# Half as many, wider reads of queries and keys, and three steps moved into the opening of an attention block

## The reference

```
mod = (silu(c) @ wmod).reshape(B, 6, 1, 256)            # shift, scale, gate for each half
sa, ca, ga, sb, cb, gb = mod[:, 0] ... mod[:, 5]
ga, gb = sign * maximum(|.|, 0.25)
h = layernorm(x) * (1 + ca) + sa
Q, K, V = h @ W_qkv.T + b_qkv, per head                 # 16 heads of 16
attn = softmax(causal(Q K^T / 4))
x = x + ga * ((attn V) @ W_o.T + b_o)
h = layernorm(x) * (1 + cb) + sb
w = softmax of the two best of h @ gate_w
x = x + gb * sum over the two best experts of w_e * (silu(h @ w1[e]) @ w2[e])
```

## Time and profile before

| | |
|---|---|
| median of 3 runs | 1039.14 us (1035.15 to 1039.42) |
| profiled execution | 1042.76 us, of which span 1041.0 us |
| busy share of PE, DVE, ACT, POOL | 88%, 70%, 56%, 34% |
| mean granted TensorE clock | 0.955 |
| DMA, mean | 106 GB/s, 110.61 MB |

### The profile page before, as it was taken

How to read it: one execution, slowest core, us unless ns; L and a number is a source line. 1 busy time by engine, 2 the same in 40 slices (tenths; PEclk the granted TensorE clock), 3 DMA queues, 4 the chain that set the end, 5 groups by cost and what they waited for, 6 DMA issues and landing times.

```text
span 1041.0 us, 19379 instructions
## 1 busy us (share of the span) xinstructions
PE 920.5 (88%) x6174; PEld 539.6 (52%) x6174; DVE 729.0 (70%) x2342; ACT 578.0 (56%) x1258; POOL 357.2 (34%) x305
## 2 busy tenths in 40 slices
PE   6798799998899999989999988778599999999990
PEld 3343445333445334544443444322498889999880
DVE  6689676879666889657789676894536675444598
ACT  3245285766585777486676647558434543434452
POOL 1521011242423125224103333003577456655530
PEclk7899799999999999999999998889899999999996
DMA  8345246236316256254365473106213323222689
GB/s 275 117 63 123 75 61 137 51 48 139 70 25 135 47 92 137 67 71 104 57 114 117 106 167 110 33 25 188 51 49 118 99 66 106 77 77 67 197 279 307
DMA packets 83171, 110.61 MB, mean 106 GB/s; under 512 B 15866, under 2 KB 56370, under 8 KB 83074
## 3 DMA queue, kind: packets, MB, share of 16 engines
q1 hardware_dynamic: 75442, 89.45, 36.9%
q0 software_dynamic: 6816, 18.62, 5.6%
q10 hardware_dynamic: 816, 1.32, 0.4%
HBM read 69.42 MB, written 35.41 MB: 101 GB/s over the span
## 4 chain that ended last, share of the span: by engine, by line
PE 58%; DVE 16%; ACT 10%; issue 6%; DMA 3%; POOL 3%; SPq 3%; another core or an unknown queue 0%; POOLq 0%; ACTq 0%; DVEq 0%
PE PO L1603 9%; PE PH L1484 9%; PE PY L1484 8%; PE PS L1583 7%; PE PM L1560 6%; ACT PR L973 4%; DVE MXF L1277 3%; PE PHT L1687 3%; PE PX L1615 2%; PE PX L1529 2%; DVE JK L1274 2%; SPq L673 2%; PE PS L1587 1%; DMA LD<-OS 1%; PE PX L1538 1%
## 5 line engine op out<-in xcount | busy, mean ns | idle before, releaser
L973 ACT ACTIVATE PR<-PS 128x512 f32<-128x512 f32 (+3 forms) x768 | 334.8, 498 | 162.1 <-PE PS L1587 125.7
L1274 DVE CUSTOM_DVE_ANT_0 JK<-PM,MK 128x128 bf16<-128x128 f32 (+3 forms) x512 | 238.6, 483 | 59.4 <-PE PM L1560 58.8
L1560 PE MATMUL PM<-QK 128*128 128x512 bf16 (+3 forms) x768 | 250.5, 335 | 27.6 <-DVE MXF L1277 15.2
L1583 PE MATMUL PS<-QK 128*128 128x512 bf16 (+3 forms) x768 | 248.5, 334 | 12.1 <-ACT PR L973 11.3
L1277 DVE TENSOR_REDUCE MXF<-PM 128x1 f32<-128x512 f32 x256 | 174.8, 683 | 75.4 <-PE PM L1560 73.8
L1603 PE MATMUL PO<-PR,V 128*17 128x512 f32 (+3 forms) x1536 | 165.2, 503 | 0.0
L1583 PEld LDWEIGHTS PS<-QK 128*128 128x128 bf16 x768 | 74.9, 98 | 173.8 <-ACT PR L973 107.8
L1560 PEld LDWEIGHTS PM<-QK 128*128 128x128 bf16 x768 | 75.5, 99 | 105.8 <-DVE MXF L1277 38.8
L1484 PE MATMUL PH<-W1S,XT 128*128 x426 | 115.2, 406 | 15.1 <-DVE XT L1446 14.0
L1033 ACT ACTIVATE HS<-PH 128x512 f32<-128x512 f32 x71 | 42.5, 598 | 142.2 <-PE PH L1484 136.0
L893 POOL DMA_INDIRECT XL<-H2D,TOK x71 | 80.6, 1135 | 115.2 <-DVE TE L1417 67.8
(11 more groups left out here) (266 smaller groups left out, 1279.8 us busy)
## 6 DMA issues: line engine op xcount, KB each, us to landing
QK<-SD SPq DMA_DIRECT2D x180, 128.0 KB
SD<-SP SPq DMA_DIRECT2D x42, 256.0 KB, 2.8
OP<-OS SPq DMA_DIRECT2D x64, 64.0 KB
LP<-LR SPq DMA_DIRECT2D x64, 64.0 KB
W1S<-in_w SPq DMA_DIRECT2D x8, 512.0 KB, 6.0
W2L<-in_w SPq DMA_DIRECT2D x4, 1024.0 KB, 7.8
X<-XA SPq DMA_DIRECT2D x3, 1024.0 KB, 8.5
H2D<-XA SPq DMA_DIRECT2D x3, 1024.0 KB, 4.6
```

Of the source, the lines that this page charges most:

```text
L973: eng.activation(PR[:, slot, i, c0:512], PS[m % 3][:, c0:512], ACT.Exp, scale=0.25).then_inc(S["exp"].sem, 1)
L1274: eng.tensor_tensor_reduce(JK[:, jk % 2, 0:w], PM[m % 3][:, 0:w], MK[:, 512 - w:512], 1.0, -3.0e38, ALU.add, ALU.max, MXA[:, mb, h, qt:qt ...
L1560: eng.matmul(PM[m % 3][:, 0:128 * (k1 - k0)], QK[:, r, h, 0, qt * 128:(qt + 1) * 128], QK[:, r, h, 1, k0 * 128:k1 * 128], start=True, stop ...
L1583: last = eng.matmul(PS[m % 3][:, c0:512], QK[:, r, h, 1, j * 128:(j + 1) * 128], QK[:, r, h, 0, 512 * f + c0:512 * f + 512], start=True, s ...
```

## The change

**Reads.** `ROWS` now has six entries (queries or keys, first block, count of blocks, first part, whether the parts differ). With one entry two or three blocks of 16 partitions are read at once: where `more` is 1, from parts that follow each other in DRAM; where it is 0, from one part that is repeated (`broadcast_to`, a dimension of step 0). So that a head's number and its row come in an order that allows this, the rows of W_qkv and b_qkv for queries and keys are reordered ahead of the kernel (`by_row`), a pair's row in SD is now number-major, head-minor, and QK is laid out as queries or keys first, then head. The stores, the count of bytes read and the matmuls stay as they are.

```
@@ -72,8 +72,8 @@
 
-ROWS = [(which, n, part) for which, parts in enumerate(((0, 0, 0, 1, 1, 2), (0, 1, 2, 0, 1, 0)))
-        for part in range(3) for n in range(6) if parts[n] == part]
+
+ROWS = ((0, 0, 3, 0, 0), (0, 3, 2, 1, 0), (1, 5, 1, 0, 1), (1, 3, 2, 0, 1), (0, 5, 1, 2, 0), (1, 0, 3, 0, 1))
 
@@ -143,14 +143,17 @@
         place(-3, 0, stats0(half) + [(0, ("mod",))] * (half == 0))
+    place(-3, 0, [(0, step) for _, step in stats(1)[:6]])
     for half in range(2):
...
             place(-3, 1, [(0, ("sd", 0, 0)), (0, ("rep", 0, 0))])
+            place(-3, 1, [(0, step) for _, step in stats(1)[6:8]])
         place(-3, 1, [(0, ("tr", 0, k, half)) for k in range(2)])
...
     place(-3, 1, [(0, ("sd", 0, 1)), (0, ("rep", 0, 1))])
+    place(0, 4, stats(1)[8:])
     for tp in range(4):
@@ -161,7 +164,7 @@
                 place(w + 1, 2 + 2 * tp, one("v", b, tp))
-        if b:
+        if b > 1:
             place(w - 1, 4, stats(b))
@@ -174,9 +177,10 @@
             place(2 * u + 2, 17, one("div", u))
-    place(0, 18, one("mod2"))
-    place(0, 20, one("gates"))
-    place(0, 22, one("bvo"))
+    for i in range(8):
+        place(0, -35, one("mod2", i))
+    place(1, 12, one("gates"))
+    place(0, -20, one("bvo"))
     for b in range(B - 1):
@@ -206,8 +210,8 @@
         for f, n in ((2, NM),) if g else ((0, NM0), (1, NM)):
-            place(g, n // 2 - LEAD, [(0.5 if g and i else 0, ("cmax", g, f, i)) for i in range(f == 0, 6)]
-                  + [(CROW if g else 2, ("crow", g, f))])
+            place(g, n // 2 - LEAD - (f == 0), [(0.5 if g and i else 0, ("cmax", g, f, i)) for i in range(f == 0, 6)]
+                  + [(CROW if g else 1 if f == 0 else 2, ("crow", g, f))])
         if g == 0:
@@ -329,8 +333,8 @@
     "sd": {"sd0": 32, "sd1": 32, "sd2": 32},
-    "rep": {"rep_a": lambda g, half: 192 * (half == 0),
-            **{f"rep{i}": (lambda g, half, i=i: (208 if g >= 3 else 192) * (slot_of(g) == i and half > 0)) for i in range(3)}},
+    "rep": {"rep_a": lambda g, half: 96 * (half == 0),
+            **{f"rep{i}": (lambda g, half, i=i: (112 if g >= 3 else 96) * (slot_of(g) == i and half > 0)) for i in range(3)}},
     "max": {"m": 1, "mx": 1},
@@ -666,12 +670,15 @@
                         sp.wait_ge(S["neg"], 3)
-                        eng.dma_start(QK[96:99, r, :, 0, :], ZR[:, :].unsqueeze(1).broadcast_to([3, 4, T])
+                        eng.dma_start(QK[96:99, r, 0, :, :], ZR[:, :].unsqueeze(1).broadcast_to([3, 4, T])
                                       ).then_inc(S[f"rep{r}"].sem, 16)
-                    for which, n, part in ROWS:
-                        sd_done(sp, u, part, half)
-                        eng.dma_start(QK[16 * n:16 * n + 16, r, :, which, sl],
-                                      SD[u, part, which, r0:r0 + 64, sl].rearrange("(h r) t -> r h t", r=16)
+                    for which, n, count, part, more in ROWS:
+                        parts = slice(part, part + 1 + more * (count - 1))
+                        for k in range(parts.start, parts.stop):
+                            sd_done(sp, u, k, half)
+                        rows = SD[u, parts, which, r0:r0 + 64, sl].rearrange("a (r h) t -> a r h t", r=16)
+                        eng.dma_start(QK[16 * n:16 * (n + count), r, which, :, sl],
+                                      rows if more else rows.broadcast_to([count, 16, 4, sl.stop - sl.start])
                                       ).then_inc(S["rep_a" if half == 0 else f"rep{r}"].sem, 16)
@@ -1485,8 +1492,8 @@
 
-            def mod_columns(WM, cols):
-                for i, col in enumerate(cols):
+            def mod_columns(WM, cols, first=0):
+                for i, col in enumerate(cols, first):
                     for k in range(2):
@@ -1502,11 +1509,15 @@
                 elif kind == "mod2":
-                    pe.wait_ge(S["wm1"], 16)
-                    px_free(pe, step)
-                    mod_columns(WM1, (256, 384, 512, 640, 0, 128, 768, 896)).then_inc(S["px"].sem, 1)
+                    i = a[0]
+                    if i == 0:
+                        pe.wait_ge(S["wm1"], 16)
+                        px_free(pe, step)
+                    last = mod_columns(WM1, (256, 384, 512, 640, 0, 128, 768, 896)[i:i + 1], i)
+                    if i == 7:
+                        last.then_inc(S["px"].sem, 1)
                 elif kind == "gates":
-                    pe.wait_ge(*after("mod2", "mod2"))
+                    pe.wait_ge(*after("mod2", "mod2", 7))
                     px_free(pe, step)
@@ -1726,11 +1737,17 @@
 
+    w_qkv, b_qkv = np.asarray(inputs["L0_attn_W_qkv"]), np.asarray(inputs["L0_attn_b_qkv"])
+
+    def by_row(a):
+
+        return a.reshape(8, 4, 16, -1).transpose(0, 2, 1, 3).reshape(a.shape)
+
     nc = bacc.Bacc("TRN2", target_bir_lowering=False, num_devices=1)
...
         "x": inputs["L0_attn_x"],
-        "wqkvT": np.asarray(inputs["L0_attn_W_qkv"]).T,
-        "b_qk": np.asarray(inputs["L0_attn_b_qkv"])[0:512].reshape(4, 128).T,
+        "wqkvT": np.concatenate([by_row(w_qkv[0:512]), w_qkv[512:768]]).T,
+        "b_qk": by_row(b_qkv[0:512]).reshape(4, 128).T,
         "b_v": np.asarray(inputs["L0_attn_b_qkv"])[512:768].reshape(2, 128).T,
```

## The result

| | before | after |
|---|---|---|
| median | 1039.28 us (4 runs, 1035.15 to 1041.12) | 1183.17 us (4 runs, 1181.81 to 1188.21) |
| ratio | | 1.142 (1.138 to 1.146) |
| profiled execution: span, mean clock | 1041.0 us, 0.955 | 1180.0 us, 0.903 |
| busy share of PE, DVE | 88%, 70% | 79%, 62% |
| share of the DMA queue of SyncE, of 16 engines | 36.9% of 1041 us | 24.8% of 1180 us |

The change makes the kernel 14% slower. The forecast was 1130, with 1057 to 1185; 1.142 of the median that it started from is 1187, at and just over the upper end. The direction and the mechanism came, the size did not: 91 us were forecast, and 144 (or 148 by the ratio) came.

What follows compares the result with a forecast made beforehand. TensorE sets the pace in the middle, VectorE in the first group. 28.6 - 10.4 = 18 us early plus 72 in later windows make 90, taking the profiled 1042.8 to 1133; forecast 1130 on the median's scale, range 1057 to 1185.

Steps and rivals of the forecast that it cites:

- That last step no row shows: New reads: the smaller side's outermost dimension decides, so 3, 2, 2 and 3 engines; a group takes 23.5 us instead of 10.9.
- rival 1: New reads: the smaller side doesn't decide, all 16 engines carry them, only the gains remain, -13 us, 1026; 13%.
- rival 2: Few engines, but a lone one reaches 30 GB/s or more; six reciprocal stalls of about 3 us; 1077, part of the 80%.
- rival 3: Few engines, but VectorE's wait doesn't reach TensorE; only the opening's 18 us remain, 1057; 4%.
- the even windows: Windows 2, 4, ... 12: LP<-LD 12.4 us later each, reciprocal waits; 54 us plus 18 of low clock, 72.
- rival 4: Whole kernel: gains and losses cancel, within 0.5% of before (5 us); 3%.
- the three banks: Even windows: TensorE can run three PSUM banks ahead, about 1.5 us each time, cutting 63 us by 9 to 54.
- the odd ones nothing, since of what VectorE waits for nothing lies behind their reads: Odd later windows: their slower reads cost no time; the later windows' 72 us come from the even ones.
- the reads of groups 0 to 3: Early reads: opening +11.3, group 1 +8.8, altogether 21.6 with the bias product's 1.5; group 2 +11.2.
- the bias product's 1.5: Opening, after 50 us: the moved bias product costs VectorE and TensorE about 1.5 us, not covered.
- the gain of the steps: Moved steps: -10.4 for second modulation part and bias product, -4.2 for sums of sequence 1, +1.5 given back; -13 us.
- the 4.2 us of the sums: First group, where VectorE sets the pace: moving the sums of sequence 1 into the opening saves 4.2 us.

Runs made afterwards that it cites:

- experiment 3: Changed kernel with the same six reads written with the 16 rows outermost from group 1 on, twelve reads for each half of group 0: 0.9931 of before.
- experiment 5: Changed kernel with reads of three blocks cut to two and one, giving four reads of two blocks and four of 16 partitions: 1.1296 of before.
- experiment 6: Changed kernel with twelve narrow reads except wide ones for groups 5, 7, ... 15 (odd windows): 1.035 of before; or for 4, 6, ... 14 (even windows): 1.0727.
- experiment 1: Changed kernel with twelve reads of 16 partitions for its six, new layout and moved steps kept: 0.9952 of before.
- experiment 7: Kernel before with all moved steps: 0.9958; only `mod2`, `gates`, `bvo`: 0.9959; only sums of sequence 1: 0.998; only reordered rows and new layout, twelve reads: 1.0038.

## Why the prediction was wrong in size

**Right: the mechanism of the slow reads.** The smaller of the two outermost dimensions sets the number of engines. LP<-LD 27.6 us behind the first read (28.1), the first maximum at 44.1 (45.85), the seventeenth at 58.9 (61.90), a wait of the reciprocal in six windows (9 to 12 us forecast, 9.5 to 14.9 seen), a DMA share near 0.2 for over 20 us at 50 to 70 GB/s (0.25 at 73): all are in the trace. "That last step no row shows" is now shown by experiment 3, and by the share of 0.13 in experiment 5. All four rivals are out: rival 1 by the share of 0.25, rival 2 by these waits where it had about 3 us, rival 3 by 81 us of the even windows, rival 4 by the ratio.

**Near: the even windows.** They were put at 72 us, 54 of TensorE's waits and 18 of clock. They cost 81 by the ratio and 76 between the two traces of experiment 6, which show the terms: TensorE idle 61 us more, and busy 15 more at the lower clock. VectorE's reciprocal waited 69 us more (73.0 for 4.4) where 63 was forecast, so the three banks gave their credit, 8 us for 9, and the clock cost nearly what it was put at; what was too low is VectorE's wait.

**Wrong: "the odd ones nothing, since of what VectorE waits for nothing lies behind their reads".** This is the step that failed, for 41 of the 57 us that are missing. The question was asked for what stands behind the reads in the queue, and not for the reads' own consumer, TensorE's first maximum of the group. For groups 1 and 2 the forecast did compare landing and due time; for the later groups it did not, though it takes one line: reads go out at place 2 of a window, the group's first maximum stands at place 14 (34 places ahead of its own window, which is the next but one), 12 places are 18.6 us where a window of 24 takes 37.15, and the reads were put at 25.6 with start and landing. That is 7 us late, and 9.2 to 9.9 were seen in windows 3, 7 and 11. There the maximum, less its wait, stood 18.9 us behind the first read and the landing took 28.2 to 28.8. In windows 5 and 9, where the list has layernorm and output steps in these places, it stood 27.4 us behind, and the waits are 0.8 and 1.0. In even windows the reciprocal stands ahead of this maximum in the list, and the trace shows no wait for the reads there.

**Near: the reads of groups 0 to 3.** 21.6 + 11.2 less the bias product's 1.5 is 31 us. The ratios leave 31, the traces show 37.9; that the first agrees to the microsecond is luck. In the trace each group's reads took 2 us more than 25.6 (group 1: issued 65.74, first maximum 93.64), the opening was 3 us later, and group 3's wait of 2.86 us had no term.

**Wrong: the gain of the steps.** -13 us forecast, -4 to -5 measured. The two waits that the move takes away were 8.5 us, but what comes last instead, the read of the row of maxima, is waited for by 1.4 us; `mod2` ahead of the first maximum makes the next row of maxima 2 to 4 us late where the reads are quick; and the 4.2 us of the sums are mostly given back. By the ratios: 9 us of steps, 9 of even windows, 41 of odd ones, less about 2 elsewhere, is 57, with an error of 4 us or so on each of the windows' terms.

## What to carry to other kernels

Before merging DMAs, look at the outermost dimension of both sides as the instruction carries it: two or three blocks put outside a dimension of 16 left three or two engines of 16, to halve a count of issues that nothing waited for. The same merge with the 16 rows outermost and the copies inside keeps all engines. When a transfer becomes slower, compare its landing with its own first reader in every window, before asking what is queued behind it.

## What the runs showed of the hardware that was not expected

- A DMA engine's pace was not one number. 25 GB/s for each of the few busy ones in the kernel after; 9 GB/s for each of 16 with destinations of 16 partitions, whether its runs are 2 KB (144 GB/s) or 8 KB long (142 GB/s, experiment 1); 12 GB/s with 48, 32 and 16 partitions (187 GB/s, experiment 3); 23 for stores to DRAM from 128. The share is near 1 in all but the first, so a share of 1 is no sign of full speed. With all 16 engines at work the reads to 48, 32 and 16 partitions were quicker than those to 16 alone; how much of the 25 is due to fewer busy engines no run separates.
- The issue of a read of half the columns depends on the layout: 12 in 5.62 us with the layout of before (experiment 7, all steps), 7.55 us in the new one (experiment 1). Both have runs of 1 KB and 16 partitions; why is open. The 7.05 of the earlier trace rows are no exception: there one read took 1.88 us to issue and the other eleven 0.43 each.
- A cost of moving `mod2` that was not in the forecast: in the kernel with only `mod2`, `gates` and `bvo` moved, one small operation of VectorE took 3.46 us where its neighbours take 0.17. It began 0.09 us after GpSimd's memset of QK, whose single steps take 3.5 us, and TensorE then waited 3.74 us for a bank:

```profile
38.55 0.17 DVE L1193 TENSOR_SCALAR MS<-MOD 128x16 f32<-128x16 f32 x1
38.66 7.07 POOL L848 MEMSET QK<- 32x4096 bf16 x2 [33.05 <-PE PM L1565]
38.75 3.46 DVE L1195 TENSOR_SCALAR MS<-MS 128x16 f32<-128x16 f32 x1
...
42.94 0.61 PE L1565 MATMUL PM<-QK 128*128 128x512 bf16 x1 [3.74 <-DVE MXA L1275]
```

The Trainium skill ("SBUF — State Buffer", Who interferes with whom) says that a tensor_scalar in one of VectorE's two-port modes and GpSimd lock each other out for a whole instruction, whoever is first, and that tensor_tensor has no such mode. The trace agrees: the operation ends 3.55 us behind the memset's start, and the TENSOR_TENSOR after it, with the second memset running, takes 0.18. Where the operation ran ahead of the memset, as in the kernel with all steps on the layout of before, it took 0.17. A run that takes the memset away was not made.
